# A gather that waits for the gather before it, in a two-layer graph network on one core

## The reference

```python
# x: 12500 nodes x 16, src/dst: 400000 edges (sorted by dst), edge_attr_16: 400000 x 16, edge_type_8: 400000
x = layernorm(x + L0(x, edge_attr_16, W_e, b_e, bias, src, dst))
x = layernorm(x + L1(x, src, dst, edge_type_8, edge_emb, w_ih, w_hh, b_ih, b_hh))

# L0: a 16x16 matrix for each edge from its attributes, applied to the source's row, mean over the destination
ew = (efeat @ W_e + b_e).reshape(E, 16, 16)
msg = einsum('ei,eio->eo', feat[src], ew)
out = segment_sum(msg, dst) / max(count, 1) + bias

# L1: one of eight 16x16 matrices for each edge by its type, summed over the destination, then a GRU cell
msg = einsum('emh,eh->em', edge_emb[edge_type].reshape(-1, 16, 16), features[src])
m = segment_sum(msg, dst)
out = gru(m, features)
```

## Time and profile before

| | us |
|---|---|
| median of 3 runs | 5807.87 (5798.56 to 5818.69) |
| the profiled execution | 5833.2 |
| its span, first to last instruction | 5831.4 |
| TensorE, VectorE, ScalarE, GpSimd busy | 5227.1, 4199.3, 3891.8, 3412.9 |
| gathers of stage 0 and 1, mean of one | 0.968, 0.959 |
| mean granted clock of TensorE | 0.979 of full speed |

### The profile page before, as it was taken

The page is one execution under the profiler, slowest core; times in us unless marked ns, Lnnn a source line. Parts: engine busy times, 40 slices in busy tenths (PEclk is TensorE's granted clock), DMA queues, the critical chain, the costliest instruction groups (busy, mean ns, idle before and its releaser), DMA issues.

```text
span 5831.4 us, 131035 instructions
## 1 busy us (share of the span) xinstructions
PE 5227.1 (90%) x41758; PEld 4693.1 (80%) x41759; DVE 4199.3 (72%) x5387; ACT 3891.8 (67%) x5533; POOL 3412.9 (59%) x3559
## 2 busy tenths in 40 slices
PE   6999999999999999999978888888888888888887
PEld 5888888888888888888767878788877788788887
DVE  7878787778777788777856666666666666666666
ACT  6666676676666666666566666666666666666664
POOL 6555565555555555555555656655655655655554
PEclk9999999999999999999989999999999999998998
DMA  3111111111111111111111111111111111111110
GB/s 66 33 30 31 33 31 31 31 31 33 30 31 33 30 31 33 31 32 31 25 23 23 23 24 23 23 23 22 23 23 23 23 23 22 24 22 23 23 23 14
DMA packets 330970, 161.25 MB, mean 28 GB/s; under 512 B 193244, under 2 KB 330011, under 8 KB 330771
## 3 DMA queue, kind: packets, MB, share of 16 engines
q1 hardware_dynamic: 218224, 130.59, 9.3%
q0 software_dynamic: 112512, 29.03, 6.3%
q10 hardware_dynamic: 160, 0.80, 0.1%
HBM read 157.44 MB, written 2.66 MB: 27 GB/s over the span
## 4 chain that ended last, share of the span: by engine, by line
PE 63%; issue 15%; DVE 12%; another core or an unknown queue 6%; DVEq 4%; ACT 0%; DMA 0%; POOL 0%; SPq 0%; ACTq 0%
PE psN L752 46%; PE psM L789 15%; DVE cand L953 6%; DVEq L997 2%; DVE nodeT L935 2%; DVE z L991 2%; DVE z L959 1%; DVEq L934 1%; DVEq L952 0%; PE psN L893 0%; PE psM L764 0%; DVEq L958 0%; PE psM L773 0%; DVE grp_hot L943 0%
## 5 line engine op out<-in xcount | busy, mean ns | idle before, releaser
L752 PE MATMUL psN<-table_hi,pick 128*128 128x320 f32 (+1 forms) x13670 | 4080.1, 316 | 167.8 <-DVE cand L953 85.3
L752 PE MATMUL psN<-table_lo,pick 128*128 128x320 f32 (+1 forms) x13670 | 3987.4, 308 | 13.7 <-issue 13.7
L752 PEld LDWEIGHTS psN<-table_hi,pick 128*128 128x128 f32 x13670 | 2598.8, 190 | 306.4 <-issue 226.1
L578 ACT ACTIVATE pick<-dist 128x640 fp32r<-128x640 bf16 (+1 forms) x2485 | 1790.5, 784 | 1336.8 <-PE psN L752 852.8
L752 PEld LDWEIGHTS psN<-table_lo,pick 128*128 128x128 f32 x13670 | 2599.6, 190 | 21.6 <-issue 21.5
L500 POOL DMA_INDIRECT z<-in_x,idx x1761 | 1704.4, 968 | 1176.9 <-issue 417.4
L500 POOL DMA_INDIRECT z<-h_rows,idx x1755 | 1682.2, 959 | 1168.3 <-issue 403.7
L570 ACT ACTIVATE dist<-src_mod,neg_node 128x640 bf16<-128x640 uint16 (+1 forms) x2485 | 1972.6, 874 | 3.3 <-DMA src_mod<-src_mod_rows 3.3
L953 DVE TENSOR_TENSOR cand<-psN,grp_hot 128x640 f32<-128x640 f32 (+1 forms) x1492 | 1122.1, 765 | 1061.3 <-PE psN L752 482.7
L991 DVE TENSOR_TENSOR z<-psD,z 128x2048 f32<-128x2048 f32 (+1 forms) x750 | 1367.8, 1824 | 55.6 <-issue 31.5
L789 PE MATMUL psM<-z,onehot 128*32 128x273 f32 (+1 forms) x12500 | 904.4, 345 | 371.4 <-issue 327.0
(11 more groups left out here) (108 smaller groups left out, 734.3 us busy)
## 6 DMA issues: line engine op xcount, KB each, us to landing
src_mod<-src_mod_rows SPq DMA_DIRECT2D x249, 192.0 KB
src_mod<-src_mod_rows SPq DMA_DIRECT2D x248, 160.0 KB
z<-in_x,idx POOLq DMA_INDIRECT x1761
z<-h_rows,idx POOLq DMA_INDIRECT x1755
eab<-in_edge_attr SPq DMA_DIRECT2D x125, 200.0 KB
idx<-in_src SPq DMA_DIRECT2D x250, 12.5 KB
dstb<-in_dst SPq DMA_DIRECT2D x250, 14.0 KB
grp<-src_grp SPq DMA_DIRECT2D x249, 5.5 KB
```

Source lines behind the costliest of these rows:

```text
L578: act.activation(pick[j][:, CHUNKS[i], 0:hi - lo], dist[i][:, 0:hi - lo], ACT.Relu, bias=1.0, scale=-1.0).then_inc(l["pick_act"], 1)
L752: mm = pe.matmul(rows[:, :, 0:cells.shape[2]], pick[j][:, c, at:at + P], cells, start=(i == 0 and part == 0), stop=(i == TC - 1 and part = ...
```

## The change

Each gather names a semaphore `gen` (one for each stage) that GpSimd raises by 1 when its engine has finished the instruction, with the descriptors written and the transfer started. Before each gather but the first of a stage stands one more wait, for the count of all gathers before it. This wait comes after the waits that the position has already.

```diff
@@ semaphores of a stage
-                hot_g=sem(f"l{k}_hot_g"), sel=sem(f"l{k}_sel"),
+                hot_g=sem(f"l{k}_hot_g"), gen=sem(f"l{k}_gen"), sel=sem(f"l{k}_sel"),
@@ def gathers(k, table)
                 l = L[k]
+                made = [0]
@@ body, after the waits of the position
                             n += 1
+                            if made[0]:
+                                pool.wait_ge(l["gen"], made[0])
                             pool.indirect_dma_start(
                                 xs[k][buf][:, g, :], None, table,
                                 bass.IndirectOffsetOnAxis(ap=idx[buf][:, g:g + 1], axis=0),
+                                engine_sem=l["gen"],
                             ).then_inc(l["got"][buf][j], 16)
+                            made[0] += 1
```

## The result

The changed kernel takes 5817.62 us (median of 20 runs, 5814.68 to 5819.35), the kernel before 5797.4 us in the same comparison (20 runs, 5789.31 to 5820.05): ratio 1.0031, interval 1.0024 to 1.0038, that is 20 us. The forecast was 102 us more than its 5807.87. One thing is needed for all that follows: the one profiled execution of the kernel before, 5833.2 us, is slower than each of its 20 runs and 36 us over their median, while that of the changed kernel, 5814.75 us, lies 3 us under its own median. So blocks of the kernel before, taken from its trace, may be some 0.15 us too long for 5797 us (36 us over 248 blocks).

The account below looks back on a forecast made before the run. TensorE was taken to set the pace until longer gaps made GpSimd the bound. Stage 0's +63 us, stage 1's +9 us and a 30 us guess gave +102 us: 5910 us, own range 5830 to 6118, 8-in-10 range 5790 to 6120.

Parts of the forecast that it names:

- What bounds the kernel now: TensorE sets the pace, busy 90%; GpSimd follows with 2324 us idle over both stages, 41% of them.
- The placing of the wait: Before gathers: the wait becomes a separate instruction at eleven of fourteen positions in stage 0, ten in stage 1.
- The size of the gap: Before a gather behind a separate wait: 0.82 us, midway between 0.75 and 0.90; 0.31 us before the others.
- The sum: GpSimd's gaps against its idle time: +63 us in stage 0, +9 us in stage 1, with a 30 us guess +102 us.
- lower end of 0.75 us: Gap before gathers of 0.08 plus 0.67 us: GpSimd has 31 and 78 us to spare, time 5808 to 5838 us.
- The guess for the interplay: Blocks of both stages in which TensorE is the later engine: 0.12 us for each of 248 blocks, 30 us.
- rival (3): TensorE's sums: spaced gathers remove a sixth of its 327.0 us idle, 55 us faster, 5753 us; chance 0.07.
- The rule cited against the sum: GpSimd's sequencer decodes on while an instruction waits, so little more than 0.16 us would be exposed before a gather.
- Rivals (1) and (2): Gap before gathers: at or under 0.75 us, chance 0.19, or 1.0 us or more, chance 0.11.
- The hidden wait: Before gathers: the gap stays at or under 0.75 us, time 5808 us within 15 us; chance 0.19.
- The late semaphore: A gather's signal comes late, gap 1.0 us or more: +540 us, with the 30 us 6378 us; chance 0.11.

Follow-up runs that it names:

- e2: Changed kernel with the new wait ahead of each position's `picked` or `mm`: 4971.27 us, ratio 1.0113 to the kernel before.
- e7: Changed kernel with the new wait only where the gather itself can carry it: 4916.2 us, ratio 1.0002 to the kernel before.
- e8: Changed kernel with each gather waiting for the gather before last instead of the last: 4915.22 us, ratio 1.0001 to the kernel before.
- e9: Kernel before with 18 extra matmuls a block in stage 0 and 32 in stage 1: 5941.72 us, ratio 1.0247 to the kernel before.
- e10: Changed kernel with 18 extra matmuls a block in stage 0 and 32 in stage 1: 5893.6 us, ratio 1.0166 to the kernel before.
- e6: Changed kernel with two more, long fulfilled wait instructions before ten gathers a block in stage 0, nine in stage 1: 6215.09 us, ratio 1.2644 to the kernel before.
- e11: Changed kernel with the new wait first at every gather, also ahead of `idx` and `free` at a block's first: 5828.34 us, ratio 1.0055 to the kernel before.
- e1: Changed kernel without the new wait, gathers only raising the semaphore: 4916.09 us, ratio 1.0 to the kernel before.

## Why the prediction was wrong

**What bounds the kernel now: right for its profile, but not a property of the kernel.** The 2324 us of idle time of GpSimd were there, but only where the kernel before takes 5797 us. With blocks of 20.30 and 18.03 us GpSimd has 6.9 and 4.6 us a block, beside the gathers' own time (20.30 - 13.4 and 18.03 - 13.4), of which 14 x 0.30 = 4.2 us are its shortest gaps and 0.3 us the rare long ones; stage 0 has 2.4 us to spare, stage 1 next to nothing.

**The placing of the wait: right.** Eleven positions of fourteen in stage 0 and ten in stage 1 got the long gap, the others 0.30 us, as forecast. e2, e7 and e8 confirm the reason from three sides: the cost goes when the gather carries the wait, when the wait is left out at those positions, and when the separate wait opens early.

**The size of the gap: the step that failed.** The sum took 0.82 us, midway between 0.75 and 0.90; it is 0.77 us in stage 0 and 0.75 in stage 1. The upper end came from the thought that 0.14 us of a gather's work might follow its recorded end and hold the signal. It doesn't: the trace records the raising of `gen` 0.01 us after that end, the wait instruction passes 0.02 us later, and the gather starts 0.74 to 0.76 us after the signal. This one term is 1355 x 0.05 = 68 us in stage 0 and 1240 x 0.07 = 87 us in stage 1. The prediction's own lower end of 0.75 us gave 5808 to 5838 us, which holds the 5817.62 measured. So the mechanism was right and the size of this term was not: the measured price lies at the lower bound, the sum of two parts read from rows (0.08 + 0.67), and I had moved the value off it for a mere possibility. Two pieces of luck are in that bound. The parts themselves were off in opposite ways, 0.01 and 0.74 to 0.76 us where rows of other instructions gave 0.08 and 0.67. And 5808 to 5838 us holds the result although it has none of the rare long gaps below (84 us): they went into what that sum had to spare, 31 and 78 us, and into the 30 us of the guess.

**The guess for the interplay: nothing where 30 us were put.** It added 30 us for blocks in which TensorE is late. There are none after the start-up blocks, since GpSimd never waits. The block of stage 1 is even shorter than in the trace of the kernel before (22.46 against 22.66 us), though 0.15 of these 0.20 us may be the slow execution. What settles it is e9 against e10: with TensorE busy for 98%, the change makes the kernel 48 us faster, so the old pace was no floor that the change had to keep. In sign and size this is rival (3) (55 us, with a chance of 0.07); in the changed kernel itself it is covered, since GpSimd sets the pace. TensorE's unexplained idle time before the sums fell as well:

```profile
PE psM L794 <- issue: 69.4, 83, 3.4
```

against 327.0 us in the earlier trace rows. But TensorE's idle time as a whole rose (its busy time fell by 71 us, the span by 18), in front of the picks and transposes, so part of it has only moved. That the spacing of the gathers is what helps is argued, not shown; e9 against e10 shows only that the change as a whole does.

**Left out of the sum: the rare long gaps**, about 0.35 us a block or some 84 us over both stages (against that, a gather of stage 0 took 0.951 us in place of 0.964, 0.19 us a block less). They come at the same gathers in every kernel that shows them. Gather 1230 of stage 0 (counted from 0) is the one at 2028.32 in the changed kernel's rows above, gap 3.05 us. The same gather in the timelines of the kernel before, e6 and e8:

```profile
2019.22 0.95 POOL L500 DMA_INDIRECT z<-in_x,idx  x1 [1.80 <-issue]
```

```profile
2180.65 0.95 POOL L510 DMA_INDIRECT z<-in_x,idx  x1 [3.22 <-issue]
```

```profile
1786.46 0.95 POOL L503 DMA_INDIRECT z<-in_x,idx  x1 [1.79 <-PE psN L757]
```

In the kernel before some of them, at gathers 203 and 483 of stage 0 for instance, are only 0.41 us, and none costs anything where GpSimd has idle time. In the changed kernel none is short: 1.80 us where the gather carries its wait, and 1.26 us longer (3.05 against 1.79) behind a closed separate wait; here it is time of the kernel. My first reading, that GpSimd loads its program there (the page's instruction transfers rose from 47 to 67 packets with the change), falls: e6 has about 1.7 times the instructions for each gather and 104 such packets, but the long gaps stand at the same gathers. So they go by the number of gathers; what they are is open. (The gaps that are 0.3 us longer do go with the instructions: about every 70th gather in the changed kernel, every 40th in e6.)

**The sum redone per block** with measured terms is that of the first section: GpSimd's own need is the block, 23.07 and 22.46 us. Against the profiled execution of the kernel before this is +0.13 and -0.20 us a block, 124 x (0.13 - 0.20) = -8 us. The profiled executions are 18 us apart (5833.2 before, 5814.75 after); the other 10 us lie outside the blocks, in the work behind the last gather (63 us before, 53 us after). The +20 us arises against the median of 20 runs, 5797.4 us, which lies 36 us under the profiled execution; the 3 runs known in advance had it only 25 us under. So that the change costs and doesn't gain hangs on two paces that lie within 1% of each other.

**The rule cited against the sum.** In e2 and e8 a gather that carries its wait for the previous gather, or stands behind a wait opened one gather earlier, starts 0.30 us after it, no later than one that waits for nothing: in e8 it stands behind a wait that was passed 1.5 us before its start. There the Trainium skill (Perfetto Trace Analysis, DMA Instruction — SWDGE (GPSIMD)), by which decoding goes on while an instruction waits, agrees. The prediction stretched this rule, which is on an instruction that waits itself, to a gather behind a separate wait instruction that is still closed. That is where the traces don't bear it out: of the 0.74 to 0.76 us from signal to start little would have been left.

**Rivals (1) and (2).** The hidden wait named 0.75 us as its limit, and 0.77 and 0.75 us sit on it; its time of 5808 us, within 15, holds the result where the forecast's own range doesn't, but this is luck, for the wait isn't hidden: it uses up all that was idle, and GpSimd's pace happens to be within 1% of the one that the kernel had. The late semaphore is excluded by the 0.01 us from a gather's end to its signal.

## What to carry to other kernels

A wait that opens at the end of the instruction just before it should be carried by the waiting instruction itself, so put it first in the list of waits: the same order then adds nothing to the gap (e2, at all but a block's first gather), where as a separate instruction it adds 0.45 to 0.47 us each time. Where one instruction earlier is enough, waiting for that is free as well (e8). Both were measured where the kernel before takes 4915 us; where it takes 5797 us the only such form that ran (e11) had the short gaps and was still 0.55% slower. When an engine's idle time is about to be used up, compare its own need for a block (so many instructions, so many shortest gaps, and its rare long ones) with the measured block, and take the price at the value that rows show directly, not midway to a possibility. And "no difference" between two bounds that are close is a coincidence of that machine: the same edit cost 0.3% here and 18% on chips where the other engine doesn't wait.

## What the hardware showed that I had not expected

- **Chips differ by 18% for this kernel.** 4915 to 4916 us on two chips, 5797.93 on another and 5797.4 in the comparison. Where it takes 4915 us, TensorE's signal that a column is picked comes 0.33 us after its last matmul's start, in all but 1 or 2% of cases; where it takes 5797 us the median is about 1.0 us and nearly six in ten are over 0.5 us (e9: about six in ten; the changed kernel there: about four in ten). One to five of a hundred such signals are missing from the trace of the kernel before, and more from that of the changed one, so these shares are rough. The granted clock doesn't explain it: 0.979 and 0.997, 2% apart. What delays the signals is open, as is whether it belongs to the chip or to something else that differed between the groups of runs, and whether it is the cause of the 18% or goes along with it.
- **A gather's own semaphore is exact**: raised 0.01 us after the recorded end, and raising it costs nothing (e1).
- **A fulfilled wait instruction is free when it is passed ahead of time**, before the gather in front has started (gap 0.30 us in e8); behind a closed wait each adds 0.085 us (e6).
- **Every 93rd or 94th gather can start late**, with a gap of 1.8 us (3.05 behind a closed wait). In the kernels whose gathers all wait for the one just before, every one of them does; in the kernel before, e1, e7 and e8 some have a gap of only 0.3 to 0.4 us.
